# Small attention on one Trainium2 core: weighted sums in four lumps, pieces on even places, a third query/key buffer, reads one round ahead, and expert weights loaded by their own stage

## The reference

```python
x = L0_attn_a_x                                   # (16, 256, 128) float32
x = x + _L0_attn_a_ref(_layernorm(x), ...)        # wide attention, 8 heads of 128
x = x + _L0_ffn_ref(_layernorm(x), ...)           # small attention, then 8 experts, top 1
x = x + _L0_attn_b_ref(_layernorm(x), ...)        # wide attention, 16 heads of 64
x = x + _L0_ffn_ref(_layernorm(x), ...)           # again
x = x + _L1_attn_a_ref(_layernorm(x), ...)        # small attention, causal, rotary
x = x + _L1_ffn_ref(_layernorm(x), ...)           # small attention, then 8 experts, top 2
x = x + _L1_attn_b_ref(_layernorm(x), ...)        # state space, small attention (causal), dense
x = x + _L1_ffn_ref(_layernorm(x), ...)           # again
```

```python
def _attention(x, Wq, bq, Wk, bk, Wv, bv, Wo, bo):
    q = (x @ Wq + bq).reshape(b, s, H, dh)
    k = (x @ Wk + bk).reshape(b, s, H, dh)
    v = (x @ Wv + bv).reshape(b, s, H, dh)
    scores = jnp.einsum('bqhd,bkhd->bhqk', q, k) / math.sqrt(dh)
    attn = jax.nn.softmax(scores, axis=-1)
    out = jnp.einsum('bhqk,bkhd->bqhd', attn, v).reshape(b, s, d)
    return out @ Wo + bo
```

## Time and profile before

| | us |
|---|---|
| median of three runs | 4938.84 |
| the profiled execution, first to last instruction (span) | 4944.1 |
| the six small attentions together, from the windows of the trace | 2034.0 |
| of these, the 14 rounds in which both scores and turned scores run | 1550.3 |

### The profile page before, as it was taken

The page is one execution under the profiler, slowest core; times in us unless marked ns, Lnnn a source line. Parts: engine busy times, 40 slices in busy tenths (PEclk is TensorE's granted clock), DMA queues, the critical chain, the costliest instruction groups (busy, mean ns, idle before and its releaser), DMA issues. The chain is left out here.

```text
span 4944.1 us, 90876 instructions
## 1 busy us (share of the span) xinstructions
PE 3835.4 (78%) x25840; PEld 2735.3 (55%) x25840; DVE 3465.1 (70%) x9524; ACT 2341.8 (47%) x5537; POOL 2386.9 (48%) x3900
## 2 busy tenths in 40 slices
PE   7889797779999799568869937567775887799365
PEld 5666565656666466456646626422332665466265
DVE  7887775666666676566658856669998664588566
ACT  3444464355666466234436624345553454366243
POOL 5666442534344442446643354367776662233453
PEclk9999898789999899679979959779998999899698
DMA  6000332100000232133323311212121330133113
GB/s 234 0 0 1 112 124 76 52 20 1 0 0 1 72 124 94 39 124 107 107 80 117 110 38 47 73 48 65 63 62 64 114 117 28 51 120 112 36 46 87
DMA packets 244547, 341.24 MB, mean 69 GB/s; under 512 B 26976, under 2 KB 187120, under 8 KB 243120
## 3 DMA queue, kind: packets, MB, share of 16 engines
q1 hardware_dynamic: 230960, 309.19, 18.8%
q0 software_dynamic: 13184, 27.22, 1.6%
HBM read 182.77 MB, written 147.26 MB: 67 GB/s over the span
## 5 line engine op out<-in xcount | busy, mean ns | idle before, releaser
L522 DVE TENSOR_REDUCE l0att_rowmax<-l0att_S 128x2 f32<-128x512 f32 x512 | 339.8, 687 | 125.2 <-PE l0att_S L701 122.9
L893 POOL TENSOR_TENSOR wb_prob<-wb_prob,wb_rden 128x128 f32<-128x128 f32 (+1 forms) x512 | 248.2, 506 | 360.7 <-DVE wb_rden L1070 360.3
L522 DVE TENSOR_REDUCE l1ffn_rowmax<-l1ffn_S 128x2 f32<-128x512 f32 x512 | 337.6, 686 | 87.2 <-PE l1ffn_S L701 83.1
L1983 POOL TENSOR_TENSOR ssm_hc<-core_AW_all,ssm_Cs 128x512 f32<-128x512 f32 x256 | 320.8, 1268 | 131.2 <-DVE core_AW_all L2129 98.1
L1434 POOL DMA_INDIRECT results<-e_y,e_back x220 | 213.7, 971 | 289.4 <-DVE e_y L1662 269.9
L935 ACT ACTIVATE wb_prob<-wb_biased,wb_nmax 128x128 f32<-128x128 f32 (+1 forms) x512 | 228.6, 447 | 236.0 <-DVE wb_nmax L1063 233.6
L2228 PE MATMUL ssm_Y<-ssm_hc,core_ident 128*128 128x512 f32 x512 | 287.8, 672 | 56.8 <-POOL ssm_hc L1983 31.1
L2129 DVE TENSOR_TENSOR_SCAN core_AW_all<-core_AW_all,ssm_U 128x512 f32<-128x512 f32 x256 | 310.6, 1213 | 1.0 <-ACT core_AW_all L2072 0.6
L701 PE MATMUL l1ffn_S<-l1ffn_K,l1ffn_Q 128*128 128x512 f32 x512 | 251.0, 494 | 75.1 <-DVE l1ffn_rowmax L522 42.3
L1775 PE MATMUL e_H<-e_xT,e_W1s 128*128 128x128 f32 x1760 | 252.0, 288 | 70.2 <-issue 50.6
L701 PE MATMUL l0att_S<-l0att_K,l0att_Q 128*128 128x512 f32 x512 | 248.6, 489 | 60.4 <-DMA l0att_K<-bounce 47.5
(11 more groups left out here) (498 smaller groups left out, 11511.3 us busy)
## 6 DMA issues: line engine op xcount, KB each, us to landing
bounce<-l0att_parts SPq DMA_DIRECT2D x128, 256.0 KB, 2.8
bounce<-l1ffn_parts SPq DMA_DIRECT2D x128, 256.0 KB, 2.8
ssm_Cs<-c_rows SPq DMA_DIRECT2D x128, 256.0 KB, 3.1
routed<-core_Y SPq DMA_DIRECT2D x8, 2048.0 KB, 24.8
l0att_Q<-bounce SPq DMA_DIRECT2D x128, 128.0 KB
l0att_K<-bounce SPq DMA_DIRECT2D x128, 128.0 KB
bounce<-l1att_parts SPq DMA_DIRECT2D x64, 256.0 KB, 2.8
l1ffn_Q<-bounce SPq DMA_DIRECT2D x128, 128.0 KB
```

The source lines that it names most:

```text
L522: dve.tensor_reduce(out=rowmax[:, jp, qt, 2 * pair:2 * pair + 2], in_=S[a % 2][:].rearrange("p (j k) -> p j k", j=2)[:, :, 0:keys(qt)], op ...
L893: ins = pool.tensor_tensor(out=prob[:, w_ % NP, a:b], in0=prob[:, w_ % NP, a:b], in1=rden[:, w_ % NP, n:n + 1].to_broadcast([P, b - a]), o ...
L1983: pool.tensor_tensor(out=hc[:, u % 4], in0=hs[:, u % 4], in1=Cs[:, n % 4], op=ALU.mult)\
```

## The change

In `small_attention`:
- `weigh` works in quarters of four matmuls, and the table `WEIGHTS` puts two quarters each at places 3 and 7 (second half of the heads, sequence r-1) and 11 and 15 (first half, sequence r).
- The pieces move: `out` to place 0 (a round later than before), `v` 2, `mt1` 3, `h` 4, queries 6, keys 8, `n0` 10, `mt0` 11, `n1` 12, `on` 14. Without rotary, queries and keys become two pieces. There is one more round at the end.
- `Q` and `K` get a third buffer, `Vp` a fourth. Half of the clearing of `K` goes from DVE to ACT (`clear_keys`).
- SP reads both halves of sequence r+2 in round r, and stores r+3 at its end. Before, it read hp 1 of r+1 and hp 0 of r+2, and stored r+2 at its beginning.
- POOL and DVE follow: `part_max` of hp 1 stands after all four masks, `normalise` a sequence further ahead, `statistics` at place 9, `finish_norm` at place 5.

In `experts`: `W1` and `W2` are allocated by the stage, SP loads them as the first thing in it, and DVE waits for them (`w_in`) where it waited for `moe_loaded`. `load_experts` and its two calls go.

```diff
-            plan = {3: "mt1", 4: "v", 5: "n0", 6: "n1", 7: "h", 9: "qk", 10: "on", 11: "mt0", 13: "out"}
+        plan = {0: "out", 2: "v", 3: "mt1", 4: "h", 6: q_piece, 8: k_piece, 10: "n0", 11: "mt0", 12: "n1", 14: "on"}
...
+    WEIGHTS = {3: (1, (0, 1)), 7: (1, (2, 3)), 11: (0, (0, 1)), 15: (0, (2, 3))}
...
             def send(n, hp):
-                await_(sp, turned, turned.at(n - 2, 8 * hp + 8))
+                await_(sp, turned, turned.at(n - BUFS, 8 * hp + 8))
...
             for r in ROUNDS:
-                if inside(r + 2) and r >= 0:
-                    store(r + 2)
-                if inside(r + 1):
-                    send(r + 1, 1)
                 if inside(r):
                     send_max(r, 1)
                 if inside(r + 2):
-                    if r < 0:
-                        store(r + 2)
                     send(r + 2, 0)
+                    send(r + 2, 1)
                 if inside(r + 1):
                     send_max(r + 1, 0)
+                if inside(r + 3):
+                    store(r + 3)
...
+            sp.dma_start(W1[:], w1.rearrange("e d f -> d e f")).then_inc(w_in.sem, 16)
+            sp.dma_start(W2[:], w2.rearrange("e (c f) d -> f e c d", f=P)).then_inc(w_in.sem, 16)
             if prefetch:
                 prefetch(sp)
...
-            dve.wait_ge(w_loaded[0], w_loaded[1])
+            dve.wait_ge(w_in.sem, 32)
```

More of the change, by code:

```diff
@@ L275, in store @@
                 sp.wait_ge(parted.sem, parted.at(n))
-                for hp in range(2):
-                    await_(sp, sent[n % 2][hp], sent[n % 2][hp].at(n // 2, 0))
+                if n >= 2:
+                    for hp in range(2):
+                        last_read = sent[(n - 2) % BUFS][hp]
+                        sp.wait_ge(last_read.sem, last_read.at((n - 2) // BUFS, SENDS))
                 for part in range(2):
@@ L424, in _ @@
             last(1)
-            for r in range(-1, SEQS + 1):
-                hide(r - 1, 12, 15)
+            normalise(2)
+            own.settle()
+            for r in range(-1, SEQS + 2):
+                hide(r - 1, 12, 16)
                 if inside(r):
                     part_max(r, 1)
-                hide(r - 1, 15, 16)
-                if inside(r + 3):
-                    normalise(r + 3)
-                hide(r, 0, 8)
+                if out_norm and inside(r - 2):
+                    out_power(r - 2)
+                hide(r, 0, 7)
                 if inside(r + 1):
                     part_max(r + 1, 0)
+                hide(r, 7, 8)
                 if inside(r + 3):
                     part(r + 3)
-                hide(r, 8, 12)
+                hide(r, 8, 11)
+                if inside(r + 4):
+                    normalise(r + 4)
+                hide(r, 11, 12)
                 last(r + 3)
-                if out_norm and inside(r - 1):
-                    out_power(r - 1)
         @block.scalar
@@ L618, in _ @@
             statistics(2)
-            for u in range(8):
+            for u in range(SLOTS):
                 after_slot(-2, u)
-            dve.memset(K[:, 1].bitcast(F32), 0.0).then_inc(zeroed[1].sem, 1)
-            for u in range(8, SLOTS):
-                after_slot(-2, u)
+            for b in range(1, BUFS):
+                dve.memset(Q[64:128, b].bitcast(F32), 0.0).then_inc(q_cleared[b].sem, 1)
             own.step(dve.memset(Vp[:, 0:2, :, :, DH:32], 0.0))
-            own.step(dve.memset(Vp[:, 2:3], 0.0))
+            own.step(dve.memset(Vp[:, 2:4], 0.0))
             own.settle()
@@ L659, in piece @@
                         pe.wait_ge(scaled.sem, 4)
-                    both = {"qk": ("q", "k"), "qq": ("q", "qr"), "kk": ("k", "kr")}[x]
-                    for m in range(2):
-                        ins = pe.matmul(F[:, m * L:(m + 1) * L], w[both[m]], hT[:], start=True, stop=True)
+                    for m, y in enumerate({"q": ("q",), "k": ("k",), "qq": ("q", "qr"), "kk": ("k", "kr")}[x]):
+                        ins = pe.matmul(F[:, m * L:(m + 1) * L], w[y], hT[:], start=True, stop=True)
                 elif x == "v":
@@ L700, in score @@
                               start=True, stop=False, skip_group_check=True)
-                ins = pe.matmul(out[:, :, 0:keys(qt)], Q[:, n % 2, jp, pair, tile(qt)],
-                                K[:, n % 2, jp, :, pair, 0:keys(qt)], start=not causal, stop=True,
+                ins = pe.matmul(out[:, :, 0:keys(qt)], Q[:, n % BUFS, jp, pair, tile(qt)],
+                                K[:, n % BUFS, jp, :, pair, 0:keys(qt)], start=not causal, stop=True,
                                 skip_group_check=causal)
@@ L1259, in _, with experts @@
             tail(TURNS - 1, 0)
-def experts(nc, core, name, *, affine, normed_in, w_loaded, gate, gate_b, act_fn, top, b1=None, b2=None,
+def experts(nc, core, name, *, affine, normed_in, w1, w2, gate, gate_b, act_fn, top, b1=None, b2=None,
             out_norm=None, out=None, prefetch=None):
```

155 lines of the change are left out of this document (81 added, 74 removed).

## The result

The changed kernel takes 5206.2 us (5204.6 to 5222.7), the kernel before 4939.9 on the same chip: 1.0545 times as long, interval 1.0528 to 1.0563. The forecast was 5143, 4990 to 5210, slower. The profiled execution has a span of 5203.4 us, 259.3 more than before.

A forecast was written before the change was run, and what follows sets the result against it. PE was taken as near its floor in the six small attentions, with waits differing by stage. Rounds +102, starts +32 and clock +70 made +204 us on the median 4938.8: 5143 us, range 4990 to 5210.

The forecast's parts named there:

- The ring: Small attentions, once per round: turned score, copy for hp 1, eight reads, copy for hp 0, turned score; 19.4 us in `l0att`.
- first turned score to the copy for hp 1, full clock: Places 0 to 3 on PE, then to SP's copy: 0.56, 0.55, 0.83, 1.64 and 0.72 us in `l0att`.
- two groups, the copy for hp 0, turned score: SP's reads in `l0att`: first group 8.62 us, second behind it 5.3, copy behind the reads to the turned score 0.45.
- The clock: PE's gap of about 3 us per round lowers the granted clock: 1.0 us in four stages, 0.5 in `l1ffn`; +70 us.
- my middle: Clock loss of 1.0 us a round in four stages, 0.5 in two, between nothing and 1.48 in each (+124 us).
- Starts: In each small attention's start the copy for sequence 0 gets a second group ahead: 6 times 5.3, +32 us.
- Lumps: Weighted sums at 3, 7, 11, 15 come later than the masks: `l1att`'s wait, about 2 us per round, goes.
- Weights: Expert stages: two loads of 2.1 MB each, 24 us, hidden by 82 us before first use; 0 to -2 us.
- the second group overlaps the first: Rival for SP's reads: if half the second group runs beside the first, rounds about 17 to 18 us, 4911 us; chance 0.05.
- PE as the bound: Rival: the copy for hp 0 doesn't wait for eight reads, rounds fall to PE's busy time; 4824 us, chance 0.11.

The follow-up runs named there:

- the three matmuls: The changed kernel with three added matmuls of constants on PE ahead of the turned score of place 0 in each round: 5110.3 us, 1.034.
- ACT's empty queue: The changed kernel with the copies of the maxima issued by ACT on its own queue instead of SP's: 5033.9 us, 1.019.
- the old reads: The changed kernel with SP's reads in the order of before (hp 1 of r+1, hp 0 of r+2): 4840.3 us, 0.979.
- the reads are short: The changed kernel, its order of reads kept, with 8 rows instead of 4 as the outermost dimension of each read: 4804.7 us, 0.972.

## Why the prediction was right, point by point

**The ring.** Its terms, predicted and measured in the first `l0att`:

| | predicted | measured |
|---|---|---|
| first turned score to the copy for hp 1, full clock | 4.30 | 4.36 |
| the copy's issue and the step behind it | 0.70 | 0.71 |
| two groups, the copy for hp 0, turned score | 14.37 | 14.23 |
| together, full clock | 19.4 | 19.3 |
| loss of clock | 1.0 | 1.67 (6.03 less 4.36) |

The ring came out as summed because each of its pieces stood in the trace of before; the rounds at full clock in the changed kernel show it, 19.5 in `l0att` and 20.5 in `l1ffn`. In the causal stages it was 19.5 at full clock and not 19.1: the 0.1 that half-width scores were to save at each of places 0 to 3 stands in no row, and with the three matmuls a causal round is at most 0.1 to 0.2 shorter than one of `l0att`.

**The clock** is the term that was mis-sized in four stages: 1.0 us a round was taken for `l0att`, `l1att` and `gqa`, while 1.4 to 1.7 were lost. The 0.5 for the two `l1ffn` was about right, 0.7 and 0.3. In `l1att` before, some rounds paid 1.48 for a gap of 2.2 us and some nothing, and I took a middle. With 2.1 us and more in every round, 64 of 84 rounds paid, some of them twice, and more than 1.48 where all of places 0 to 2, which lie on the ring, ran slowly. With 1.67 in each round of the six the rounds would come to 110.74 + 7.26 + 10.0 = 128; measured are 1772.9 / 14 = 126.6. The Trainium skill, page "TensorE: Matmul & The Clock Gate", section "Why this matters for your kernels", names idle gaps as what drops the clock. By that alone every round would pay (5197), which came nearer than my middle but is not what the rounds show. That the gap is what costs, the three added matmuls bear out.

**The mechanism of the ring** was right in its effect and for the most part wrong in one of its reasons. The copy does come late beside the reads issued ahead of it; that it does so because it stands behind them in one queue is the smaller part: from ACT's empty queue it still landed after 5.9 us, where 7.0 were measured behind the reads and 2.3 without them. I had the row that could have told me, 26% of the engines during a group, and read it as a limit of the reads, not as four engines of 16 that the copy, four rows too, would have to share.

**Starts.** 32 us were predicted; starts and ends together grew by 12. The first wait of each stage is 4.9 to 5.5 us, but it lies in the windows of rounds 0 to 13, whose later rounds wait 2 to 5 us too.

**Lumps.** The waits of the earlier trace rows went, as said; the gain shows only where the ring doesn't hide it, 2.9 us a round in `l1att` with the old reads.

**Weights.** Hidden as argued: +2.6 us, within the measurement. The 3.5 us at the first scatters were missed, too small to matter; the first copy of `W1` starts some 87 us into the stage, where 82 were expected.

**What was not in the sum:** `wb`, +17 us. It moved the time from 5189 to the upper edge of the range.

**How near the sum came by luck.** With the clock's part taken out by the three matmuls, the six windows sum to 1673.8 us, 119.6 for a round of all six where 118.0 were summed: the ring was 22 us too short, the clock 29, and the starts were 20 too long. `wb`, the experts and the rest add 25. That the ring and the starts cancel is luck; about 55 us are left between +204 and the measured +259.

**The rivals.** That the second group overlaps the first: refuted, 5.2 to 6.2 us where 5.3 were predicted. PE as the bound: it is what the kernel becomes once the reads are short, and 4804.7 is close to the 4824 of that case.

## What to carry to other kernels

Before reads are moved ahead, follow each small DMA that may share engines with them and that the next round waits for: behind eight reads issued just before it, it landed about 7 us after its issue instead of 2.3, in every round. Look at the share of DMA engines while one kind of transfer is in flight; where it is a plain fraction (0.25), try whether the shape of the transfer sets it, as it did here: another order of its dimensions can be worth more than the whole change (here 5206 to 4805 us with one line). And where a stage that was not touched gets longer, look at the packets of the instruction queues in it.

## What the runs showed of the hardware that I had not expected

- A DMA of 16 KB on a queue of its own landed 5.9 us after its issue in the median and let PE go on after 7.4 in the longest case, beside eight reads of another queue; issued by SP with no reads ahead, it took 2.7 us with the ACT step in it.
- The place of a DVE loop of 337 instructions in the program is worth 17 us: in each of the five middle passes five packets of 8 KB are fetched, or none.
- Work added on PE, three matmuls a round, made the kernel 96 us faster than the changed kernel; the granted clock was 0.99 instead of 0.91 in the first `l0att`.
